# Projection steps of a two-layer attention pipeline dealt anew to head groups, and softmax sums inverted from PSUM

## The reference

```python
x = rmsnorm(x, ln1_w)
kv_d, q_d = x @ kv_d_w, x @ q_d_w                    # latents, 128 wide
k_p, q_p, v = kv_d @ k_u_w, q_d @ q_u_w, kv_d @ v_u_w
k_r, q_r = rope(x @ rope_k_w), rope(q_d @ rope_q_w)
k, q = concat([k_p, k_r]), concat([q_p, q_r])        # 16 heads of 16 + 16
probs = softmax(where(causal, q @ k.T * scale, min))
out = (probs @ v) @ o_w
```

## Time and profile before

| | us |
|---|---|
| median of 3 runs (lowest, highest) | 2436.31 (2430.26, 2440.63) |
| the profiled execution's own time | 2439.99 |
| its span, first to last instruction | 2437.9 |
| mean granted TensorE clock, share of full | 0.942 |
| last copy of a group's output (end of the head groups) | 1707.3 |

### The profile page before, as it was taken

One profiled execution on the slowest core, in us unless ns is written; L12 is line 12 of the kernel. 1 busy time (PEld: TensorE's weight loads), 2 busy tenths in 40 slices (PEclk: granted clock), 3 DMA queues, 4 the chain that ended last, 5 costly groups with the idle time before them and its releaser, 6 DMA issues. The chain is left out here.

```text
span 2437.9 us, 38264 instructions
## 1 busy us (share of the span) xinstructions
PE 2154.7 (88%) x12880; PEld 1526.5 (63%) x12880; DVE 1552.7 (64%) x4272; ACT 1092.7 (45%) x2230; POOL 1065.4 (44%) x1092
## 2 busy tenths in 40 slices
PE   5898988999898899988899989898488899999994
PEld 4575554766655576654656756564266688888873
DVE  5666666666676766667667665664365556556557
ACT  2344553434454434445444344543233355555543
POOL 1455454444555354555454553544045133333323
PEclk9899999999999999999999998996699899999996
DMA  5544546553555544544645545333548687787796
GB/s 161 170 125 143 141 147 198 142 146 108 154 147 184 157 139 138 154 143 130 200 122 148 174 140 141 94 88 104 181 159 283 220 198 188 202 211 193 190 272 228
DMA packets 226527, 399.99 MB, mean 164 GB/s; under 512 B 25118, under 2 KB 95646, under 8 KB 222238
## 3 DMA queue, kind: packets, MB, share of 16 engines
q1 hardware_dynamic: 162590, 297.86, 40.9%
q0 software_dynamic: 17792, 39.99, 8.4%
q10 hardware_dynamic: 45952, 59.71, 6.8%
HBM read 147.85 MB, written 148.44 MB: 122 GB/s over the span
## 5 line engine op out<-in xcount | busy, mean ns | idle before, releaser
L726 ACT ACTIVATE probs<-scoresT 128x512 f32<-128x512 f32 (+3 forms) x1024 | 425.9, 439 | 453.7 <-PE scoresT L1189 439.1
L941 DVE CUSTOM_DVE_ANT_0 unused<-score,mask 128x128 bf16<-128x128 f32 (+3 forms) x1024 | 466.7, 486 | 250.7 <-PE score L1166 230.1
L1189 PE MATMUL scoresT<-stacks 97*128 97x256 f32 (+2 forms) x1024 | 402.2, 409 | 42.8 <-DMA stacks<-negmax 22.4
L641 POOL TENSOR_TENSOR probs<-probs 128x1536 f32<-128x1536 f32 (+1 forms) x128 | 379.2, 2962 | 26.1 <-PE out_ps L1203 15.4
L1166 PE MATMUL score<-stacks 96*128 96x256 f32 (+2 forms) x1024 | 349.0, 385 | 42.3 <-DVE rowmax L941 39.6
L630 POOL TENSOR_SCALAR_AFFINE_SELECT probs<-probs 128x512 f32<-128x512 f32 x256 | 165.7, 647 | 421.7 <-ACT probs L726 421.7
L1189 PEld LDWEIGHTS scoresT<-stacks 97*128 97x128 f32 x1024 | 195.0, 194 | 171.8 <-ACT probs L726 83.8
L1166 PEld LDWEIGHTS score<-stacks 96*128 96x128 f32 x1024 | 180.9, 193 | 172.7 <-issue 113.0
L954 DVE RECIPROCAL total<-total 128x128 f32<-128x128 f32 x256 | 237.5, 938 | 79.3 <-ACT whole L737 76.1
L1829 POOL DMA_INDIRECT h_summed<-y,goal x88 | 141.9, 1613 | 292.2 <-ACT y L1925 272.0
L1226 PE MATMUL middle<-wo,outT 128*128 128x512 f32 x512 | 263.2, 604 | 1.1 <-DVEq L892 1.1
(11 more groups left out here) (197 smaller groups left out, 4124.6 us busy)
## 6 DMA issues: line engine op xcount, KB each, us to landing
stacks<-parts SPq DMA_DIRECT2D x768, 128.0 KB, 2.4
x_slots<-mask ACTq DMA_DIRECT2D x56, 1032.0 KB, 4.9
xr<-x_slots SPq DMA_DIRECT2D x22, 1032.0 KB
wturn<-parts_kept SPq DMA_DIRECT2D x7, 2048.0 KB, 8.8
raw<-in_gates SPq DMA_DIRECT2D x24, 512.0 KB
raw<-in_ups SPq DMA_DIRECT2D x24, 512.0 KB
raw<-in_downs SPq DMA_DIRECT2D x24, 512.0 KB
normed<-in_L_attn_x SPq DMA_DIRECT2D x8, 1024.0 KB, 8.3
```

The source lines that it names most:

```text
L641: pool.tensor_tensor(probs[0][:, :, P * j:T], probs[0][:, :, P * j:T], probs[j][:, :, :], ALU.add)\
L726: act.activation(probs[j][:, h, 0:width], scoresT[:, u % ST_BANKS, first:first + width], ACT.Exp, scale=SCALE).then_inc(exp_done, 1)
L941: ins = dve.tensor_tensor_reduce(unused[t][:, :], score.bank(name)[:, first:first + width], mask[:, T - width:T], 1.0, MASKED, ALU.add, AL ...
L1189: pe.matmul(scoresT[:, u % ST_BANKS, 0:T - first], heads[0:ROWMAX + 1, 1, h, j * P:(j + 1) * P], heads[0:ROWMAX + 1, 0, h, first:T], start ...
```

## The change

The lists of `projections_between` are written anew by kind:

- Kinds 1 and 2: Y(f, 3) with YN(2), X1(1), XR(0) moves from g = 1 to g = 0. V(c, 2) moves from g = 0 to g = 1. WO and the four XT move from g = 2 to the end of g = 1, and in kind 2 also LAT(p, 1). In g = 1 the `room` steps are two of 6144 columns instead of 1536 each. In g = 2, LAT comes before KR.
- Kind 3: WO and XT move from g = 2 to g = 1, P of group n + 5 from g = 3 to g = 2, V(p, 0) from g = 2 to g = 3. The load WT for the next first-layer pair moves from kind 2, g = 3, to the head of kind 3, g = 1. XL comes behind NL.
- Kind 0 keeps its lists but for the places of LS.

ScalarE no longer copies `sum_ps`. It copies the output as soon as the product with V is done, VectorE's reciprocal reads `sum_ps` and writes `total`, and TensorE's next `sums` waits for the reciprocals. The four waits that the copy covered are written out.

```diff
+LS_AT = (4, 9, 14, 18)
+G1_AT = {1: (6, 12), 2: (4, 8)}
+ROOMS = {1: 2, 2: 2}
+ROOM = 12 * T
...
+    f, p, n = c - 1, c + 1, NG * c
+    ends, starts, kind = c > 0, c + 1 < cores, c % 4
+    room = ("room", ROOM)
+    y = [quarters("Y", f, t) for t in range(TT)] if ends else [[]] * TT
...
     if g == 0:
+        if kind in (0, 3):
...
+        first = rows_of_group(n + 2) if kind == 2 else []
+        return first + y[0] + y[1] + [("YN", f, 0)] + y[2] + [("YN", f, 1), ("X1", f, 0)] + y[3] + [
+            ("YN", f, 2), ("X1", f, 1), ("XR", f, 0)]
     if g == 1:
         own = rows_of_group(n + 3)
+        if kind in (0, 3):
+            turned = [("WT", p)] if starts and kind == 3 else []
+            steps = turned + quarters("V", c, 3) + y[3] + own + ([("HS", f)] if ends else [])
+            if load:
+                steps[3:3] = load[4]
+                steps[7:7] = load[5]
+            if starts and kind == 3:
+                steps += [("WO", c)] + [("XT", p, k) for k in range(CT)]
+            return steps
+        values = quarters("V", c, 2) + quarters("V", c, 3)
+        turned = [("WT", p)] if kind == 1 else []
+        ahead = values + turned + own
+        a, b = G1_AT[kind]
+        steps = ahead[:a] + [("YN", f, 3), ("X1", f, 2), ("XR", f, 1)] + ahead[a:b] + [
+            ("X1", f, 3), ("XS", f), ("XR", f, 2)] + ahead[b:] + [room] * ROOMS[kind] + [("XR", f, 3), ("WO", c)]
+        steps += [("XT", p, k) for k in range(CT)]
+        if kind == 2:
+            steps += quarters("LAT", p, 1)
         return steps
     if g == 2:
+        if kind in (1, 2):
+            keys = quarters("KR", p, 0) + quarters("KR", p, 1)
+            q, k = quarters("P", n + 4, 0), quarters("KU", n + 4)
+            written = [("XI", f, t) for t in range(TT)] + [("IS", f)]
+            if kind == 1:
+                return (quarters("LAT", p, 1) + keys[:4] + written + keys[4:] + q + quarters("LAT", p, 0) + k)
+            return quarters("LAT", p, 0) + q + keys[:4] + written + keys[4:] + k
+        if not starts:
+            return []
+        if kind == 3:
+            return rows_of_group(n + 4) + rows_of_group(n + 5)
+        return [("WO", c)] + [("XT", p, k) for k in range(CT)] + rows_of_group(n + 4) + quarters("V", p, 0)
+    steps = [("NL", p + 1)] if p + 1 < cores and kind in (2, 3) else []
+    steps += [("XL", p)]
+    if starts and kind in (1, 2):
+        steps += rows_of_group(n + 5) + quarters("V", p, 0) + quarters("V", p, 1)
+    elif starts and kind == 3:
+        steps += quarters("V", p, 0) + rows_of_group(n + 6) + quarters("V", p, 1)
+    elif starts:
+        steps += rows_of_group(n + 5) + rows_of_group(n + 6) + quarters("V", p, 1)
     return steps
...
                     a = core_of(p)[1]
-                    last = ("V", p - 1, 3) if a == 1 else ("LAT", p - 1, 0)
-                    sp.wait_ge(*middle.full(last))
+                    for last in ([("V", p - 1, 3)] if a == 1 else [("LAT", p - 1, 0), ("KR", p - 1, 1)]):
+                        sp.wait_ge(*middle.full(last))
...
                 def close(n):
+                    pool.wait_ge(taken, n + 1)
...
-                    act.wait_ge(sum_done, n + 1)
-                    act.activation(total[:, :], sum_ps[:, :], ACT.Copy)
+                    act.wait_ge(pv_done, TT * (n + 1))
                     act.activation(whole[:, :], out_ps[:, :], ACT.Copy).then_inc(taken, 1)
...
                     if t == 0:
-                        dve.wait_ge(taken, n + 1)
-                    dve.reciprocal(total[:, mine], total[:, mine]).then_inc(inverted, 1)
+                        dve.wait_ge(sum_done, n + 1)
+                        if n % NG > 0:
+                            dve.wait_ge(out_done, closed_by_pool(n))
+                        elif n > 0:
+                            dve.wait_ge(last_done, TT * (n // NG))
+                    dve.reciprocal(total[:, mine], sum_ps[:, mine]).then_inc(inverted, 1)
...
+                    if t == 0:
+                        dve.wait_ge(taken, n + 1)
                     dve.wait_ge(inverted, TT * n + t + 1)
...
                 def latents(p, m, c):
+
                     name = "LAT", p, m
+                    if m == 1 and c == 0:
+                        turned_in(p)
+                        for k in (CT - 2, CT - 1):
+                            pe.wait_ge(*middle.out(("XT", p, k)))
...
                 def rotated_keys(p, pair, k):
                     name = "KR", p, pair
-                    if pair == 0 and k == 0:
-                        turned_in(p)
-                        for c in (CT - 2, CT - 1):
-                            pe.wait_ge(*middle.out(("XT", p, c)))
...
                     pe.wait_ge(added, 2 * (n + 1))
+                    if n > 0:
+                        pe.wait_ge(inverted, TT * n)
```

More of the change, by code:

```diff
@@ L110, in projections_between @@
 def projections_between(c, g, cores):
[L112 to L116, removed]
-    if g == 0:
[L118 to L135, removed]
+    f, p, n = c - 1, c + 1, NG * c
@@ new lines, in projections_between @@
+    ends, starts, kind = c > 0, c + 1 < cores, c % 4
+    room = ("room", ROOM)
+    y = [quarters("Y", f, t) for t in range(TT)] if ends else [[]] * TT
+    load = []
+    if starts and kind in (0, 3):
+        load = [[("LS", p, 0)], [("LS", p, 1)], [("LS", p, 2)], [("LS", p, 3), ("LR", p)], [("LN", p, 0), ("LN", p, 1)],
+                [("LN", p, 2), ("LN", p, 3)]]
+    if g == 0:
+        if kind in (0, 3):
+            first = rows_of_group(n + 2) if kind == 3 or c == 0 else []
+            if c == 0:
+                first = first + [("WS", k) for k in range(CT)] + [("WK",)]
+            steps = first + quarters("V", c, 2) + y[0] + y[1] + y[2]
+            for at, one in reversed(list(zip(LS_AT, load))):
+                steps[at:at] = one
+            return steps
+        first = rows_of_group(n + 2) if kind == 2 else []
+        return first + y[0] + y[1] + [("YN", f, 0)] + y[2] + [("YN", f, 1), ("X1", f, 0)] + y[3] + [
+            ("YN", f, 2), ("X1", f, 1), ("XR", f, 0)]
@@ L136, in projections_between @@
     if g == 1:
-        early = quarters("V", c, 3)
-        if starts and start_layer == 1 and core_of(c)[1] == 0:
-            early += [("WT", p)]
         own = rows_of_group(n + 3)
[L141 to L153, removed]
@@ L154, in projections_between @@
-        if starts and start_layer == 0:
-            steps[3:3] = [("LN", p, 0), ("LN", p, 1)]
-            steps[7:7] = [("LN", p, 2), ("LN", p, 3)]
+        if kind in (0, 3):
[6 more added lines that the diff above has]
+                steps += [("WO", c)] + [("XT", p, k) for k in range(CT)]
+            return steps
```

## The result

The changed kernel takes **2375.99 us** in the median of 4 runs (2375.28 to 2378.49), the kernel before 2433.74 beside it (2430.26 to 2440.63). The ratio is 0.9761, 95% interval 0.9736 to 0.9786: 58 us, or 2.4%, faster. The forecast was 2368, faster with 0.86. The profiled execution of after has a span of 2373.6 us and a mean granted clock of 0.953 (0.942 before).

The account below looks back on a forecast made before the run. TensorE's matmul sequence was taken to bound the kernel, with 207 us of stillness and lowered clock to win; terms (a) to (g) summed to -68 us, giving 2368 us against a median of 2436.31, range 2330 to 2420.

Parts of the forecast that it names:

- (a): Kind 2, g = 3: spreading the loads ends the late landing of negated maxima before kind 3, g = 0; -22 us.
- (b): Kinds 1 and 3, g = 1: earlier query projections remove waits for rotated rows; -12 us and -4 us.
- (d): Kinds 1 and 2, g = 1: moving part of the norm chains makes VectorE late less often for row maxima; -9 us.
- (c): Kinds 1 and 2, g = 2: moving the x transposes off the group head removes waits for low parts; -16 us.
- (e): Group heads: without ScalarE's copy of the sums, reciprocals read the bank and exponentials start sooner; -8 us.
- (f): Crowded groups, kinds 1 and 2, g = 1: granted clock partly returns as the waits behind its fall end; -11 us.
- (g): Kinds 1 and 2: new waits from XI and XR ahead of exponentials and from a late second KR; +14 us.
- the partial return: Rival, chance 0.15: ended waits come back in part as the next ones on the same engine; 2400 us.
- The moved DMA wait: Rival, chance 0.06: the load moved to kind 3, g = 1 delays negated maxima there, (a) is lost; 2390 us.
- The slower case: Rival, chance 0.07: in kinds 1 and 2, g = 0, ScalarE's queue holds up the negated maxima; 2452 us.

Follow-up runs that it names:

- queries-first experiment: Changed kernel with the query and key projection of kind 0, g = 1 put ahead of Y: 2380.28 us, ratio 0.9776 to the kernel before.

## Why the prediction was right, and where it was not

The direction and the size were right, 58 us where 65 to 68 were summed, and so was the mechanism in (a), (b) and (d). Terms (c), (e) and (f) were not, and (g) was too low. That the total came so close is in part luck: (c), (e) and (g) together fell short by 27 us, and the clock came back in groups where none was forecast. Term by term:

- **(a) the spread loads, -22.** Right. The waits for the landing fell from 20.8 to 3.2 us, and the three groups are 22.5 us shorter together (the one shown from 32.40 to 24.70). Alone it gave 22 to 25 us. It is the largest part of the change. The longest landing is 3.9 us, where 2 to 3 were forecast.
- **(b) queries before transposes, -16.** Right as a wait: 27.0 to 12.0 us. The experiment on kind 0 removed the wait there in the same way. In kind 3, g = 1, though, a wait of 1.5 us for row maxima now stands where 1.5 us for rotated rows stood, so those 4 us did not reach the group.
- **(c) the x transposes, -16: mis-sized.** The waits for low parts fell from 18.5 to 5.8 us, not to the 2 forecast, and XT now meets the end of the XR chain, where waits of 9.0 us for normed rows took the place. Net it was worth about 4 us. I had looked at what follows XT and not at what it needs.
- **(d) VectorE's crowded groups, -9.** Right: 30.9 to 19.3 us, less 2.4 more for the last maxima. Those are in kind 3, g = 1 and 2; in g = 0 they stayed at 1.0 us each.
- **(e) reciprocals from the bank, -8: wrong.** The step that failed was "of TensorE's 14.4 us of waits for exponentials I take -8". With the old lists the exponentials gave back 2.5 us and the landing of the negated maxima took 7.0. The runs show 5 to 6 us with the old lists, at the edge of what can be told, and none with the new ones, where the longest waits for exponentials are for XR. The price of the reciprocal itself was taken right: 938 ns and 938 ns. The rule of the Trainium skill (VectorE: DVE Perf Modes, the section on the TRN2 errata), 65 ns more from a bank, does not show in these rows.
- **(f) clock, -11: wrong in its place.** The granted clock of the steady part rose from 0.96 to 0.97, from 63 to 43 us lost, with the part that belongs to (a). (A loss is the length of a stretch times the share of the clock that is missing. The 63 us are what the lower level costs; at 1.00 or 0.50 the engine was at 1.2 GHz for twice as long, 126 us, where the prediction says 63.) But the crowded groups that the term names did not gain. Kinds 1 and 2, g = 1, lost 24 us to the clock before, by the traces, and 31 after; kind 2, g = 1 fell from 0.87 to between 0.78 and 0.88, and when the long wait there was taken away it had 0.82 to 0.87. "It fell behind the waits" holds for kind 3, g = 0 and not here. The clock came back in the groups next to them: kind 1, g = 2 and 3, and kind 2, g = 2, lost 13 us before and nothing after. Room in front of XT raised it in the crowded groups too. What lowers it in kind 2, g = 1 stays open.
- **(g) new waits, +14: mis-sized.** It came to 21 us. XR in front of the exponentials was put at 0.7 us in eight groups; it is nothing in kind 1, where V has 12288 columns, and 3.7 in kind 2, where V has 4096. That V's columns cover it was not tried by itself. The XI piece costs 0.7 (forecast 1.2) and the late KR 0.8 (forecast 1).

Of the rivals, the partial return describes terms (c) and (e), and in kind 3, g = 1 a part of (b). In its working, half-way between 2368 and 2418 is 2393, not 2400. The moved DMA wait is real but small for this load: g = 2 of kind 3 lost 2 to 3 us in each pair when the load alone was moved. It came in full where a store was moved by the queries-first experiment, on SyncE's queue against a copy on ScalarE's, as the Trainium skill has it (DMA: Bandwidth & Descriptors, Issuing engines are not separate DMA queues); the trace agrees, 4.9 us to land instead of 1.8. The slower case did not come: TensorE waited at most 0.8 us for the negated maxima.

## What to carry to other kernels

Look first for the small transfer that a whole group waits for, and for the bulk transfers that are issued just before it: moving one load gave nearly half of this change, and issuing one store 8 us later took away the wait that had eaten another change. When a step moves, price what it needs at the new place as well as what waited for it at the old one. Letting an engine start sooner gains only up to the next thing that is due at the same time. And before a clock is blamed on a wait, compare groups of the same kind in one trace: here they differed by nearly 3 us with the same waits.

## What the runs showed that I had not expected

The same kernel differs from series to series: the kernel before had medians of 2417.53, 2435.00 and 2431.84 us, the first two with the same chip number on record, so only ratios within one series could be used for differences of less than 20 us. The traces show where: behind the last group's copy, in the experts that no edit touches, the four traces of the first series take 712 to 716 us and all others 728 to 731. Why is not known. The reciprocal costs the same from a bank and from SBUF, 938 ns for 128 x 128. The addition with both inputs in SBUF costs 944 or 670 ns with no change to it, only to its place in the order.
